# A transformer block with mixture of experts on one core: the row array emptied only behind each expert's last row, two accumulators, selection on the logits, routing chain and tail reordered

## The reference

```
mod = (_silu(c) @ wmod).reshape(2, 6, 1, 256)
sa, ca, ga, sb, cb, gb = (mod[:, i] for i in range(6))
ga, gb = sign(g) * max(|g|, 0.25) for both
x = x + ga * attention_block(_layernorm(x) * (1 + ca) + sa)     # ends in h + mlp
h = _layernorm(x) * (1 + cb) + sb
scores = softmax(h @ gate_weight.T)                             # 16 experts
topk_weight, topk_idx = top_k(scores, 4)                        # not renormalised
y = sum over e of w_e[:, None] * glu(h, gate_up[e], down[e])    # 176 hidden channels each
y = y + glu(h, shared_gate_up, shared_down)                     # 352 hidden channels
x = x + gb * y
```

## Time and profile before

| what | value |
|---|---|
| median of 3 runs | 453.19 us |
| the profiled execution itself | 453.05 us |
| its span in the trace | 451.3 us |
| mean granted TensorE clock | 0.868 |
| TensorE busy, share of the span | 321.8 us, 71% |
| GpSimd busy | 173.9 us, 39% |
| data moved | 65.87 MB |

### The profile page before, as it was taken

How to read it: one execution, slowest core, us unless ns; L and a number is a source line. 1 busy time by engine, 2 the same in 40 slices (tenths; PEclk the granted TensorE clock), 3 DMA queues, 4 the chain that set the end, 5 groups by cost and what they waited for, 6 DMA issues and landing times.

```text
span 451.3 us, 5495 instructions
## 1 busy us (share of the span) xinstructions
PE 321.8 (71%) x1410; PEld 236.2 (52%) x1410; DVE 209.2 (46%) x582; ACT 176.4 (39%) x341; POOL 173.9 (39%) x160
## 2 busy tenths in 40 slices
PE   6940000089989999989997476719999999999500
PEld 4730000046566668877785465516777777777300
DVE  4830000089868676428546268203434343434137
ACT  2700000289779775532642341103444444444200
POOL 3560000026791001005254765621666666665600
PEclk9995555589999999999999668858999999999955
DMA  7799999951210007711039911233676767775692
GB/s 222 286 313 356 326 327 325 336 171 50 91 49 0 0 2 209 144 21 35 2 82 328 260 52 67 92 105 77 112 113 114 112 114 110 116 112 75 112 325 97
DMA packets 62456, 65.87 MB, mean 146 GB/s; under 512 B 3163, under 2 KB 58459, under 8 KB 62427
## 3 DMA queue, kind: packets, MB, share of 16 engines
q1 hardware_dynamic: 32923, 30.89, 24.4%
q10 hardware_dynamic: 21200, 23.74, 16.2%
q0 software_dynamic: 8304, 10.88, 15.1%
HBM read 29.84 MB, written 35.67 MB: 145 GB/s over the span
## 4 chain that ended last, share of the span: by engine, by line
issue 30%; PE 25%; POOL 23%; DVE 7%; DMA 6%; ACT 4%; ACTq 3%; SPq 1%; POOLq 1%; DVEq 0%
POOL acc_rows L511 16%; POOL xs_rows L500 5%; PE ps L1528 3%; PE ps L1533 3%; PE ps L1529 3%; PE ps L1294 3%; ACTq L774 3%; PE ps L1311 3%; PE ps L1295 2%; DMA acc_rows<-w,ids 2%; DMA w<-acc_rows 2%; DMA w<-in_wmod 1%; POOL wsm_lo L405 1%; DVE b_lo L884 1%; PE ps L1329 1%
## 5 line engine op out<-in xcount | busy, mean ns | idle before, releaser
L511 POOL DMA_INDIRECT acc_rows<-w,ids x47 | 73.4, 1561 | 57.6 <-ACT w L834 57.3
L1694 PE MATMUL ps<-wup,w 128*128 x188 | 65.6, 473 | 0.5 <-issue 0.5
L1329 PE MATMUL ps<-b_hi,wsm_hi 128*128 128x512 f32 x8 | 4.3, 533 | 63.1 <-ACT b_hi L645 63.1
L1239 DVE TENSOR_TENSOR sg<-sg,ps 128x176 f32<-128x176 f32 x47 | 15.9, 338 | 71.7 <-ACT sg L826 71.7
L1720 PE MATMUL ps<-wdown,w 88*128 x188 | 48.6, 381 | 0.7 <-DVE w L1247 0.6
L542 ACT ACT_TABLE_LOAD x17 | 21.8, 1283 | 65.6 <-issue 64.7
L475 POOL TENSOR_SCALAR rr<-mv 128x4 f32<-128x4 f32 x6 | 2.1, 349 | 112.3 <-DVE mv L865 112.3
L500 POOL DMA_INDIRECT xs_rows<-h3x,slots x32 | 33.8, 1055 | 26.6 <-issue 20.0
L1694 PEld LDWEIGHTS ps<-wup,w 128*128 128x128 f32 x188 | 33.1, 196 | 11.5 <-issue 1.9
L884 DVE TENSOR_TENSOR b_lo<-ps,b_hi 128x512 fp32r<-128x512 f32 x8 | 5.5, 691 | 69.9 <-ACT b_hi L645 66.0
L834 ACT ACTIVATE w<-ps,wv 128x256 f32<-128x256 f32 x47 | 22.2, 473 | 37.0 <-PE ps L1720 37.0
(11 more groups left out here) (274 smaller groups left out, 740.4 us busy)
## 6 DMA issues: line engine op xcount, KB each, us to landing
xs_rows<-xt ACTq DMA_DIRECT2D x1, 18576.0 KB, 60.8
xt<-xs_rows SPq DMA_DIRECT2D x47, 144.0 KB, 2.2
wup<-in_wmoe SPq DMA_DIRECT2D x4, 1408.0 KB
acc_rows<-xt ACTq DMA_DIRECT2D x4, 1152.0 KB, 12.9
w<-acc_rows SPq DMA_DIRECT2D x8, 512.0 KB, 6.4
wdown<-in_wmoe SPq DMA_DIRECT2D x1, 2816.0 KB
wdown<-in_wff SPq DMA_DIRECT2D x4, 512.0 KB, 8.2
w<-in_wsm SPq DMA_DIRECT2D x3, 512.0 KB, 9.1
```

The source lines that it names most:

```text
L511: nc.gpsimd.indirect_dma_start(acc_rows[n][:, :], bass.IndirectOffsetOnAxis(ids[:, i:i + 1], 0), ysb[n], None, compute_op=ALU.add).then_in ...
L1694: last = mm(bank(1, i)[:, 0:2 * FE].rearrange("p (w n) -> p w n", w=2), xT[i % 2][:, k * P:(k + 1) * P], up[:, k, :, bass.ds(e, FE)], star ...
```

## The change

All of it in the kernel itself; the inputs are laid out as before.

- xs_rows gets room for 128 rows more per expert (SPACE = CAP + P). It is no longer filled as a whole. SP empties the last 128 rows for the dummy tile, and, once the counts are known (ends_ready), the 128 rows behind the last row of each of the 16 experts, with a row number read from a table. The tile loads wait for these (emptied).
- Two accumulators in place of four, with four buffers for the results in SBUF (YBUF). SP fills the accumulators with zeros, behind the loads of the shared expert's weights. Add i waits for the landing of add i-2.
- The gate ga goes into the copy behind the last step down (acc, scale), for which chan makes it for channels too (8 products instead of 6). hm * ga + x is made ahead, in a step pre. gated3 and plus_x are gone.
- The choice of four experts is made on the logits less their maximum (in lgsub); the exponential and the sum only feed the weights (topk), which rank no longer waits for.
- h3 is shared between ScalarE (c = 0) and VectorE (c = 1); rows.1 uses sequence 0's bank and comes earlier; eup is split into eg and ev; the plans are in another order.
- Tail: two loads per sequence, each with a semaphore of its own; the first accumulator is multiplied and added to hm while the second is on its way.

```diff
+SPACE = CAP + P
+DUMMY = NE * SPACE
-NACC = 4
+NACC = 2
+YBUF = 4
...
 SCALAR_PLAN
-    wsm.3 wsm.4 q.0 fill xconv.0 sqk.0 sqv.0 ig.0 rk.0 rv.0 ga.0 wsm.5 ...
+    wsm.3 wsm.4 q.0 xconv.0 sqk.0 sqv.0 ig.0 rk.0 rv.0 ga.0 wsm.5 ...
...
         @block.sync
+            sp.wait_ge(s("fill_ready"), 1)
+            sp.dma_start(xs_rows[1 + DUMMY:XROWS, :], empty).then_inc(s("emptied"), 16)
+            for n in range(NACC):
+                sp.dma_start(acc_rows[n][:, :].rearrange("(r p) c -> p r c", p=P),
+                             empty[:, 0:C].unsqueeze(1).broadcast_to([P, AROWS // P, C])).then_inc(s("filled"), 16)
...
+            sp.wait_ge(s("ends_ready"), 1)
+            for e in range(NE):
+                row = nc.sync.value_load(ends[0:1, e:e + 1], min_val=1 + SPACE * e, max_val=1 + SPACE * e + CAP)
+                sp.dma_start(xs_rows[bass.ds(row, P), :], empty).then_inc(s("emptied"), 16)
+
+            sp.wait_ge(s("emptied"), 16 * (NE + 1))
             sp.wait_ge(s("scattered"), 16 * NB * NT * TOPK)
...
             def scatter(b, j):
-                    pool.wait_ge(s("filled"), 16 * (1 + NACC))
...
             def acc(b):
-                    nc.scalar.activation(W[b][3][:, c, :], PB(b)[:, c, :], ACT.Copy).then_inc(s("wo_sb"), 1)
+                    nc.scalar.activation(W[b][3][:, c, :], PB(b)[:, c, :], ACT.Copy,
+                                         scale=gbc[:, KC + c, b:b + 1]).then_inc(s("wo_sb"), 1)
...
-            def fill():
-                act.wait_ge(s("fill_ready"), 1)
-                act.dma_start(xs_rows[1:XROWS, :].rearrange("(r p) c -> p r c", p=P),
-                              empty.unsqueeze(1).broadcast_to([P, XROWS // P, RW])).then_inc(s("filled"), 16)
-                for n in range(NACC):
-                    act.dma_start(acc_rows[n][:, :].rearrange("(r p) c -> p r c", p=P),
-                                  empty[:, 0:C].unsqueeze(1).broadcast_to([P, AROWS // P, C])).then_inc(s("filled"), 16)
...
             def y_out(i):
-                if i >= NACC:
-                    act.wait_ge(added[i % NACC], 16 * (i // NACC))
+                if i >= YBUF:
+                    act.wait_ge(added[i % NACC], 16 * ((i - YBUF) // NACC + 1))
...
+            def pre(b):
+                link(nc.vector.tensor_tensor(hm[b][:, :, :], hm[b][:, :, :], per_token(b, 2), ALU.mult))
+                dve.wait_ge(s("x_again"), 16 * (b + 1))
+                at["x", b] = done(nc.vector.tensor_tensor(hm[b][:, :, :], hm[b][:, :, :], tok(W[b][0]), ALU.add))
...
             def lgsub(b):
-                nc.vector.tensor_tensor(rep[b][:, :, 0:NE], lg, top8[b][:, :, 0:1].broadcast_to([P, NT, NE]),
+                nc.vector.tensor_tensor(sc[b][:, :, 0:NE], lg, top8[b][:, :, 0:1].broadcast_to([P, NT, NE]),
                                         ALU.subtract).then_inc(s("lg_sub"), 1)
+                nc.vector.tensor_copy(cut[b][:, :, TOPK:8], sc[b][:, :, NE:NE + 4])
+                link(nc.vector.tensor_tensor(cut[b][:, :, 0:TOPK], top8[b][:, :, 0:TOPK],
+                                             top8[b][:, :, 0:1].broadcast_to([P, NT, TOPK]), ALU.subtract))
+                    at_ = done(nc.vector.match_replace(rep[b][:, t, :], cut[b][:, t, :], sc[b][:, t, :], 1.0))
+                nc.vector.tensor_scalar(picked[b][:, :, :], rep[b][:, :, 0:NE], 0.0, None,
+                                        ALU.is_gt).then_inc(s("picked_ready"), 1)
...
             def chan():
-                for j in range(3 * KC):
+                for j in range(4 * KC):
...
             tail on DVE
+            for b in range(NB):
+                dve.wait_ge(acc_in[b], 16)
+                link(nc.vector.tensor_tensor(tok(W[b][0]), tok(W[b][0]), row(b, NT), ALU.mult))
+                at["hm", b] = done(nc.vector.tensor_tensor(hm[b][:, :, :], hm[b][:, :, :], tok(W[b][0]), ALU.add))
+            for b in range(NB):
+                dve.wait_ge(acc_in[NB + b], 16)
+                for h in range(2):
+                    link(nc.vector.tensor_tensor(tok(W[b][1])[:, r, :], tok(W[b][1])[:, r, :], row(b, 2), ALU.mult))
+                    nc.vector.tensor_tensor(hm[b][:, r, :], hm[b][:, r, :], tok(W[b][1])[:, r, :],
+                                            ALU.add).then_inc(s("y_ready"), 1)
```

More of the change, by code:

```diff
@@ L86 @@
     hidlo.0.1 o1.1 sqe.1 osig.1 prod.0.3 gated.1 outlo.1 hidlo.0.2 hidlo.0.3 wo.1 prod.0.4 var2.1 hidlo.0.4 prod.0.5
-    hn2.1 hidlo.0.5 prod.0.6 h2lo.1 hidlo.0.6 prod.0.7 hidlo.0.7 prod.1.0 prod.1.1 hidlo.1.0 sum3.0 gated3.0 hidlo.1.1
-    prod.1.2 plus_x.0 var3.0 hidlo.1.2 prod.1.3 hn3.0 hidlo.1.3 prod.1.4 prod.1.5 h3lo.0 hidlo.1.4 lgsub.0 prod.1.6
-    hidlo.1.5 topk.0 hidlo.1.6 prod.1.7 rank.0 hidlo.1.7 egated.0.0 sum3.1 gated3.1 elo.0.0 plus_x.1 var3.1 egated.0.1
-    hn3.1 elo.0.1 egated.0.2 h3lo.1 lgsub.1 elo.0.2 topk.1 egated.1.0 rank.1 table sum.0 elo.1.0 egated.1.1 finish.0
-    elo.1.1 egated.1.2 elo.1.2 sum.1 finish.1
+    hn2.1 hidlo.0.5 prod.0.6 h2lo.1 hidlo.0.6 pre.0 prod.0.7 hidlo.0.7 prod.1.0 prod.1.1 hidlo.1.0 sum3.0 var3.0 hn3.0
+    hidlo.1.1 prod.1.2 hidlo.1.2 prod.1.3 h3.0 hidlo.1.3 prod.1.4 lgsub.0 pre.1 hidlo.1.4 prod.1.5 topk.0 rank.0
+    hidlo.1.5 prod.1.6 h3lo.0 hidlo.1.6 prod.1.7 hidlo.1.7 sum3.1 var3.1 egated.0.0 hn3.1 elo.0.0 egated.0.1 h3.1 elo.0.1
+    egated.0.2 lgsub.1 elo.0.2 topk.1 sum.0 h3lo.1 rank.1 table egated.1.0
+    elo.1.0 egated.1.1 elo.1.1 finish.0 egated.1.2 elo.1.2 sum.1 finish.1
 """
@@ L159, in adaln_block_kernel @@
         top8 = [sb(f"top8{b}", [P, NT, 8]) for b in range(NB)]
+        cut = [sb(f"cut{b}", [P, NT, 8]) for b in range(NB)]
+        ends = sb("ends", [P, NE], I32)
         sc = [sb(f"sc{b}", [P, NT, NE + 4]) for b in range(NB)]
@@ L267, in adaln_block_kernel @@
         added = [sem(f"added{i}") for i in range(NACC)]
-        acc_in = [sem(f"acc_in{i}") for i in range(NACC)]
+        acc_in = [sem(f"acc_in{i}") for i in range(NB * NACC)]
         CH = [("ff", i) for i in range(NCH_FF)] + [("out", i) for i in range(NCH_OUT)]
@@ L557, in _ @@
             table(LOG_SET)
-            def to_high_and_full(b, hi, full, ps, scale, bias, ready):
-                for c in range(KC):
-                    nc.scalar.activation(full(c), ps[:, c, :], ACT.Identity, scale=scale(c), bias=bias(c))
-                    nc.scalar.activation(hi[:, c, :], ps[:, c, :], ACT.Identity, scale=scale(c),
-                                         bias=bias(c)).then_inc(s(ready), 1)
             def wsm_high(m):
@@ L808, in _ @@
                 "sqo": sqo, "ro": ro, "gated": gated, "wo": wo, "h2": h2, "silu": silu, "hid": hid, "acc": acc,
-                "h3": h3, "exp": exp, "ehigh": moe_high, "fill": fill, "rows": rows, "sum": sum_out, "esilu": moe_silu, "ehid": moe_hid,
+                "h3": h3, "exp": exp, "ehigh": moe_high, "rows": rows, "sum": sum_out, "esilu": moe_silu, "ehid": moe_hid,
             }
@@ L1219, in _ @@
                 "o1": o1, "osig": osig, "sqe": sqe, "gated": gated, "outlo": outlo, "wo": wo, "var2": var2, "hn2": hn2, "h2lo": h2lo,
-                "prod": prod, "hidlo": hidlo, "sum3": sum3, "gated3": gated3, "plus_x": plus_x, "var3": var3, "hn3": hn3, "h3lo": h3lo, "lgsub": lgsub, "topk": topk,
+                "prod": prod, "hidlo": hidlo, "pre": pre, "sum3": sum3, "var3": var3, "h3": h3, "hn3": hn3, "h3lo": h3lo, "lgsub": lgsub, "topk": topk,
                 "egated": moe_gated, "elo": moe_lo, "rank": rank, "table": table, "sum": sum_out, "finish": finish,
```

182 lines of the change are left out of this document (89 added, 93 removed).

## The result

The changed kernel takes 387.81 us (median of 4 runs, 385.54 to 389.70) where the kernel before takes 453.27 beside it: the ratio is 0.8536, with a 95% interval of 0.8471 to 0.8601. A second set gave 385.30 (6 runs) and 0.849 (0.8457 to 0.8523). Predicted were 382.8 and a range of 375.5 to 391. The median lies 5.0 above the forecast: inside the range, but outside the 377 to 387 that had 72%. The profiled execution took 385.54, the lowest of its four, and its span is 383.7. Before it was 451.3, so 67.6 us are gone where 70.25 were forecast. Each ratio leaves out executions more than 1.5% above the fastest of their set; there are two, one of a_elo and one of a_rstd, and a_rstd's profile is of that one.

What follows compares the result with a forecast made beforehand. ScalarE, held by the accumulator fill's issue behind 18576 KB of zeros, was taken to stall the rest for a seventh of the span. 453.05 - 63.15 + 0.2 - 3.0 - 4.3 = 382.8 us; range for 8 in 10: 375.5 to 391.

Steps and rivals of the forecast that it cites:

- Part 1: Start of the kernel: with the fill off ScalarE its stall goes and all behind moves earlier, net -63.15 us.
- Parts 2 and 3: Feed-forward layer: +0.2 us for pre.0; sequence 0's routing: slots.0 at 225.9 where it was 230.7.
- Part 4: Sequence 1's rstd on GpSimd, behind 12 scatters and a 1.8 us drain wait: rstd.1.3 ends at 248.8 against 251.64.
- the first long drain lasts as before: Routing rival, 12% together with emptying colliding with the second batch: the long first drain stays 6.20 us, time 387.
- Part 5: Sequence 1's routing: TensorE idle some 7 us for elo.0.0, 1.3 for rows.1, slots.1 at 268.3 rather than 271.27.
- Part 6: Second batch of scatters: keeps its length, the 16 emptying transfers hidden beside it, so -3.0 us.
- Part 7: Tile loop: TensorE sets the 2.465 us beat, adds have 1.1 us of slack with two accumulators, so 0.
- Part 8: Tail after the last add: fewer loads, the first taking 5.9 us from its issue; -4.3 us, between -2.5 and -6.

Runs made afterwards that it cites:

- a_elo: The changed kernel with VectorE's elo.0.0 moved ahead of the norm hn3.1; 386.94 us, ratio 0.8473.
- a_rstd: The changed kernel with GpSimd's rstd.1.3 moved ahead of elow.2 and the third four scatters; 381.77 us, ratio 0.8383.
- b_acc_sp: The kernel before with only the four small accumulator fills moved from ScalarE's queue to SP's, the large fill left on ScalarE; 394.63 us, ratio 0.8668.
- b_pieces: The kernel before with the large fill in five 3.7 MB pieces on SP, each behind a weight chunk, and accumulator fills on SP; 403.92 us, ratio 0.8888.
- b_fill_sp: The kernel before with all five fills moved from ScalarE's queue to SP's, behind the raw loads; 426.42 us, ratio 0.9385.
- a_fill_sp: The changed kernel with the whole row array filled on SP instead of the 16 emptying transfers, scatters waiting for it; 412.91 us, ratio 0.9074.
- a_held: a_three with SP's up weights held until elow.2 is done; 382.81 us, ratio 0.8398.
- a_three: The changed kernel with rstd.1.3 ahead of elow.2 and the third four scatters, elo.0.0 ahead of hn3.1, rows.1 ahead of the last four scatters; 380.67 us, ratio 0.8365.

## Why the prediction was right, and which of its terms were not

The large term, the fill, was right in size and reason. The rest was to bring 7.1 us and brought 4.2: the tail gave a little more than forecast, and the routing lost where it should have gained.

**Part 1** is right to 0.3 us (-63.15, measured -63.41). The five slices at 0 are the fourth to the eighth, not from the sixth on as the prediction counts, and the weight chunks land in 6.4 us rather than 4; neither enters the sum, as no engine waits for that chunk. Its reason, an issue that cannot be placed behind the large fill, is shown by b_acc_sp, which keeps the fill. What the prediction did not ask is what the smaller number of bytes is worth. By b_acc_sp, and the 4.0 us that the stretch up to the first scatter loses there beside the fill, it is a few us, not 60. And the fill may not stand ahead of a load that is wanted: b_pieces and b_fill_sp take 9 and 32 us more than b_acc_sp by that, a_fill_sp 25 to 28 more than the changed kernel.

**Parts 2 and 3** failed. pre.0 and the rest of the feed-forward layer were given +0.2. The trace has TensorE waiting 2.52 for hidlo.1.1, behind a norm that waited 1.47 and then took 1.41 more than undisturbed. With the shift of part 1 the first scatter was to come at 226.9 in the times of before and came at 229.6. The wait seems to be carried on whole, as SP's up weights start 3.6 later than forecast; no run takes it away, so its share is argued and not shown.

**Part 4**: rstd.1.3 at 252.2 in the times of before, not 248.8. The late first scatter is 2.7 of that, the drain, given 1.8 and measured at 4.24, is 2.4, and 1.7 come back, 1.3 of them gaps that had been added and were not there. The rival "the first long drain lasts as before" was half true. a_held shows that the up weights make it long, a_rstd that the order of GpSimd's steps is what makes it cost.

**Part 5**: TensorE's wait was right in place and size (7.43), and a_elo shows that without it TensorE still waits 4.92 for the norm and that the 2.2 us gained up to the second batch are lost in the batch. The price for rows.1 beside lgsub was too low. It was forecast from 257.3 on and began at 263.2 in the times of before, for the late rstd and for a drain at the fifteenth scatter of 5.84 us, before 2.09, that had no term of its own. 1.3 was put in for one operation, and two were held, by 1.23 and 1.39 over their undisturbed times. The prediction read the Trainium skill (SBUF - State Buffer, "Who interferes with whom") for operations with two inputs alone. The same section has copies, casts and tensor_scalar take the shared ports too, in a two-port mode, where their operands allow it. The rows fit that: a copy (1.40 for 0.17), a tensor_scalar (1.59 for 0.20) and in a_rstd the cast of slots (2.13 for 0.17) were held, while the subtraction from PSUM beside them took 0.22. The norm of sequence 0 in parts 2 and 3, a tensor_scalar that took 2.88 for 1.47 beside L419, looks the same, and took 3.14 beside it in a_three. slots.1 was forecast at 268.3 and came at 273.3: 3.4 of the 5.0 are from parts 3 and 4, the rest is here.

**Part 6**: the emptying is hidden, as a_fill_sp shows, but the -3.0 was not there. The second batch begins 2.0 us later than before instead of 2.8 earlier, and gives 1.0 back that was not forecast (26.10 for 27.12). From the tanh of ig to the first tile load the changed kernel takes 205.87 us, the kernel before 204.85. So the reordered routing as a whole costs 1.0 instead of gaining 2.8, and this is the step of the prediction that failed: 3.8 us. a_rstd shows where the gain could have been had: with rstd of sequence 1 behind eight scatters, as before the change, 4.1 us come back.

**Part 7**: nothing, as forecast, but by luck. The loop is as long as before to 0.1 us, while the hand-over of 0.8 leaves 0.3 us of the slack of 1.1 that was named, and four adds waited for a landing, 5.5 us in sum.

**Part 8**: from the last scaled y to the last y_ready it is 19.12 us, before 24.09: -4.97, forecast -4.3. The loads are quicker than the 5.9 from the issue, 4.81, and the landing that lets them go, of the last add but one, is 0.5 later than forecast. The last add is 1.3 later for its accumulator, but VectorE's first four operations cover it.

Together: -63.41 + 1.02 - 4.97, and -0.25 for the loop and the end of the span, is -67.6. The errors were -0.3 in part 1, +3.8 in the routing and -0.7 in the tail. The other 2.3 us between forecast and median are the spread: the profiled execution is the lowest of its set. That the median comes to the 387 of the rival with the long first drain is luck: the drain gives 2.4 us of the 5.0, and the rest has other sources.

## What to carry to other kernels

Look at what stands behind a long transfer on its own queue, not at its size: the issue of the large one took 0.42 us and the next one 54. Before a reorder is credited with a gain, write down every step that it puts in front of the instruction on the critical path, the drains of an indirect queue among them. A transfer that others must wait out has a period of landing plus hand-over; take the hand-over from a run in which it binds.
